# A first half's choice made earlier, a mixture's front reordered, and row loads six pairs ahead

## The reference, cut to what matters

```
x = layernorm(x + recurrent(x))            # a scan over time, sigmoid gate, projection
x = layernorm(x + cross_attention(x, ctx))
scores  = sigmoid(x @ w_gate.T)            # 16 experts in 4 groups
allowed = the 2 groups whose best two scores sum highest
idx     = top 4 experts among the allowed  # the choice
w       = scores[idx] / sum(scores[idx])
routed  = sum_k w_k * (silu(x @ w1[idx_k].T) * (x @ w3[idx_k].T)) @ w2[idx_k].T
shared  = (silu(x @ w1_s.T) * (x @ w3_s.T)) @ w2_s.T      # every token
out     = layernorm(x + routed + shared)
```

## Time and profile before

| what | value |
|---|---|
| timed runs | 1370.61, 1376.79, 1378.01 us (median 1376.79) |
| the profiled execution's own time | 1360.66 us |
| its span, first to last instruction | 1358.9 us |
| TensorE, mean granted clock over the span | 0.922 |
| busy: PE, DVE, ACT, POOL | 86%, 53%, 43%, 37% |

### The profile page before, as it was taken

One profiled execution on the slowest core, in us unless ns is written; L12 is line 12 of the kernel. 1 busy time (PEld: TensorE's weight loads), 2 busy tenths in 40 slices (PEclk: granted clock), 3 DMA queues, 4 the chain that ended last, 5 costly groups with the idle time before them and its releaser, 6 DMA issues. The chain is left out here.

```text
span 1358.9 us, 23999 instructions
## 1 busy us (share of the span) xinstructions
PE 1165.4 (86%) x7558; PEld 839.3 (62%) x7558; DVE 715.5 (53%) x1906; ACT 585.8 (43%) x1064; POOL 501.6 (37%) x924
## 2 busy tenths in 40 slices
PE   7589899899877967999999999995988676999970
PEld 3244344444344434889999999884555555998850
DVE  4767567676444644423223223285776636655564
ACT  1257677777765643223233233233333122556710
POOL 6333312331421331013333323112321278838856
PEclk9579999999998998999999999997999677999995
DMA  3980000000000007401111111032500024767633
GB/s 139 313 320 2 1 0 0 1 0 0 2 0 1 1 1 283 156 24 40 33 39 40 36 37 39 25 125 74 192 1 0 5 74 139 233 196 213 213 117 101
DMA packets 68127, 109.31 MB, mean 80 GB/s; under 512 B 7345, under 2 KB 54962, under 8 KB 65202
## 3 DMA queue, kind: packets, MB, share of 16 engines
q1 hardware_dynamic: 58130, 80.96, 17.4%
q0 software_dynamic: 9888, 27.01, 6.2%
HBM read 65.61 MB, written 42.34 MB: 79 GB/s over the span
## 5 line engine op out<-in xcount | busy, mean ns | idle before, releaser
L1391 ACT ACTIVATE f_work<-f_bank,f_ub 128x128 f32<-128x128 f32 x312 | 89.0, 368 | 204.3 <-PE f_bank L1713 204.3
L494 ACT ACTIVATE att_PT<-att_ST 128x1024 f32<-128x1024 f32 (+1 forms) x192 | 147.8, 809 | 66.3 <-PE att_ST L608 34.8
L527 DVE CUSTOM_DVE_ANT_0 att_junk<-att_RB,att_causal_q 128x128 f32<-128x128 f32 (+3 forms) x256 | 120.9, 487 | 60.7 <-PE att_RB L590 48.7
L1713 PEld LDWEIGHTS f_bank<-f_work,f_xTf 128*128 128x128 f32 x1248 | 145.4, 192 | 3.9 <-DVE f_work L1513 2.0
L1713 PE MATMUL f_bank<-f_work,f_xTf 128*128 128x128 f32 x1248 | 145.9, 276 | 1.5 <-DVE f_work L1513 1.5
L590 PE MATMUL att_RB<-att_kT,att_qT 96*128 96x512 bf16 (+3 forms) x384 | 122.0, 357 | 23.3 <-DVE att_mx L527 7.2
L1722 PE MATMUL f_bank<-wd_down,f_work 128*128 x624 | 141.2, 380 | 0.0
L1722 PEld LDWEIGHTS f_bank<-wd_down,f_work 128*128 128x128 f32 x624 | 115.8, 191 | 13.8
L1342 POOL DMA_INDIRECT Yd<-f_work,f_inv x39 | 38.5, 987 | 196.3 <-DVE f_work L1532 196.3
L1522 DVE COPY f_xTf<-wu_up 128x1024 f32 x78 | 54.1, 694 | 102.8 <-PE f_bank L1713 95.0
L590 PEld LDWEIGHTS att_RB<-att_kT,att_qT 96*128 96x128 bf16 x384 | 34.0, 99 | 115.9 <-issue 40.4
(11 more groups left out here) (456 smaller groups left out, 2230.9 us busy)
## 6 DMA issues: line engine op xcount, KB each, us to landing
Xd<-g_zero SPq DMA_DIRECT2D x1, 12032.0 KB, 38.4
f_xin<-Xd SPq DMA_DIRECT2D x47, 256.0 KB, 3.6
Yd<-f_yo SPq DMA_DIRECT2D x47, 256.0 KB, 2.2
wu_up<-up_w SPq DMA_DIRECT2D x9, 1024.0 KB, 14.4
wd_down<-down_w SPq DMA_DIRECT2D x9, 1024.0 KB, 18.4
w_all<-w SPq DMA_DIRECT2D x6, 768.0 KB, 10.8
wu_up<-Yd SPq DMA_DIRECT2D x16, 256.0 KB, 5.8
w_all<-w SPq DMA_DIRECT2D x1, 2304.0 KB, 17.3
```

The source lines that it names most:

```text
L494: act.activation(buf[:, :, 0:w], ST[:, 2 * (k % 2):2 * (k % 2) + 2, 0:w], ACT.Exp, scale=float(HD) ** -0.5).then_inc(exp_done, 1)
L527: dve.tensor_tensor_reduce(junk[:, k % RING, 0:w], RB[:, bank, 0:w], G.causal_q[:, 512 - w:512], 1.0, LOWEST, ALU.add, ALU.max, to).then_i ...
L1391: last = act.activation(hT[:, u % 2, m, :], bank[:, UB + m // 4, (m % 4) * P:(m % 4 + 1) * P], ACT.Gelu, bias=ub[:, ds(e, 1), m])
L1713: mm = pe.matmul(bank[:, UB + n, P * m:P * (m + 1)], staged_up[:, kk, at:at + P], xT[:, u % 2, kk, :], start=(kk == 0), stop=(kk == KD - 1))
```

## The change

The kernel computes the same. Work moves, and a few waits with it:

```diff
-    put(("r", 3, 1), ("tg", 0, 0), ("tg", 0, 1), ("tg", 1, 0), ("tg", 1, 1), ("lg", 0, 0))
-    put(("rs", 3, 1), ("c", 0, 0))
-    put(("y", 3, 1), ("c", 0, 1))
-    put(("tx", 3, 1), ("c", 0, 2))
-    put(("s", 3, 0), ("c", 0, 3), ("ct", 0, 0))
-    put(("dn", 3, 0), ("lc", 0, 0), ("sx", 0, 2))
+    put(("tx", 2, 1), ("tg", 0, 0), ("tg", 0, 1), ("tg", 1, 0), ("tg", 1, 1))
+    put(("v", 3, 1), ("lg", 0, 0), ("c", 0, 0), ("c", 0, 1), ("c", 0, 2), ("c", 0, 3))
+    put(("r", 3, 1), ("ct", 0, 0))
+    put(("rs", 3, 1), ("lc", 0, 0), ("sx", 0, 3))
+    put(("y", 3, 1), ("sx", 3, 13))
...
-    SCATTERS, SENT = TH * K, 2
+    SCATTERS, SENT = TH * K, 13
...
-            for q in range(N + NX):
+            LAG = 6
+            for q in range(N + LAG):
                 if q < N:
                     load(q)
-                if q >= NX:
-                    keep_result(q - NX)
+                if q >= LAG:
+                    keep_result(q - LAG)
...
+            for q in range(3):
+                stage(q)
             for m in range(2 * FIRST):
                 shared_silu(m)
-            for q in range(3):
-                stage(q)
...
-            dve.wait_ge(exp_done, 1)
-            for m in range(2 * FIRST):
-                shared_product(m)
-                route.choose(dve, ch, 1, m)
-            shared_sum(0)
-            dve.wait_ge(sums_ready, 1)
-            route.locate(dve, ch, 1, bank[:, SB_ + 1, 0:CE], bank[:, SB_ + 1, CE:2 * CE])
-            route.owners(dve, ch, 1)
-            shared_sum(1)
-            for n in range(HALVES):
-                route.weights_of(dve, ch, n)
...
             for q in range(3):
                 stage(q)
+            dve.wait_ge(exp_done, 1)
+            route.choose(dve, ch, 1, 0)
+            route.choose(dve, ch, 1, 1)
+            shared_product(0)
+            route.choose(dve, ch, 1, 2)
+            shared_product(1)
+            route.choose(dve, ch, 1, 3)
+            shared_product(2)
+            dve.wait_ge(sums_ready, 1)
+            route.locate(dve, ch, 1, bank[:, SB_ + 1, 0:CE], bank[:, SB_ + 1, CE:2 * CE])
+            shared_sum(0)
+            shared_product(3)
             take_x(0)
             take_x(1)
+            shared_sum(1)
+            route.owners(dve, ch, 1)
...
+                if q in (4, 6):
+                    route.weights_of(dve, ch, (q - 4) // 2)
...
                 if q >= 2:
                     pe.wait_ge(y_done, q - 1)
+                else:
+                    pe.wait_ge(sh_added, 2 * (FIRST - 1) + q + 1)
...
             shared_up(2)
+            count()
             shared_down(0)
             shared_up(3)
-            count()
-            shared_down(1)
             pe.wait_ge(sh_prod, 2 * FIRST)
-            pe.wait_ge(sh_added, 2 * FIRST)
-            pe.wait_ge(pos_ready, 2)
-
             turn_x(0)
             turn_x(1)
+            shared_down(1)
             up(0)
```

## The result

| | before | after |
|---|---|---|
| timed runs, median | 1374.31 us (4 runs, 1370.61 to 1378.01) | 1341.80 us (4 runs, 1341.20 to 1342.71) |
| the profiled execution's own time | 1360.66 us | 1341.20 us |
| its span, mean granted clock | 1358.9 us, 0.922 | 1339.4 us, 0.923 |

The ratio of the timed runs is 0.9763, with an interval of 0.9736 to 0.979: faster by 2.4%. The two ways of counting disagree: 32.5 us by the timed medians, 19.5 us by the profiled executions, for which the working had said 20.6.

The account below looks back on a forecast made before the run. Mixture 2's pair loop was taken to wait for POOL's scatter queue, then late loads. Terms -10.8 (including +1.7), -1.6 and -8.2 sum to -20.6 us: 1340.1 profiled, 1356 from the timed 1376.79; range 1345 to 1368.

Parts of the forecast that it names:

- Theory L: Experiments' theory: late loads cost the kernel before more in most executions than in the profiled one; the change removes that.
- Rival F: Experiments' rival to Theory L: the timed runs' excess over the profiled execution has nothing to do with the loads.
- 1, boundary later: Recurrent program: choosing ahead delays y(3), most is given back in the last quarter, and the end comes 1.7 us later.
- 3, up(0): Mixture 2's front: 11 fewer scatters after the boundary and TensorE ready in time bring up(0) 10.8 us sooner.
- 4, up(0) to third up: Start of the pair loop: TensorE stays warm, saving 1.6 us, or 0 if cold again.
- 5, loop: Pair loop: loads six pairs ahead in SP's program remove all eight stalls, saving 8.2 us.
- down(1) at the full clock: Front, now on the path: 3.6 us instead of 5.23; with turns also slow, up(0) gains only 8.6 us.
- Three staging copies beside the scatters: VectorE copies during first-half scatters: taken at nothing; by the skill's rule 1.7 us in all, 1358 us.
- A: Front gives little: part 1's 6.6 us not given back, lower clock stays; 1363 us, chance 0.13.
- B: Pair loop: contention with gathers keeps loads late, so 8.2 us stay; 1364 us, chance 0.10.
- D: Recurrent program: y(3) so late that it ends over 8 us later; some 1371 us, chance 0.04.
- C: POOL becomes the bound: 2.2 us slack remains, stretched first-half gathers eat the gain; 1384 us, chance 0.03.

Follow-up runs that it names:

- e7_lag3: The changed kernel with loads three pairs ahead of the stores instead of six: 1465.9 us, ratio 1.0767.
- c0_before: The kernel before, unedited, profiled again on another chip: 1361.8 us (one run).
- c3_before: The kernel before, unedited, timed against itself and profiled on a further chip: 1361.9 us against 1362.4.
- e1_lag_only: The kernel before with only the loads moved, six pairs ahead of the stores instead of four: 1358.4 us, ratio 0.9968.
- e4_after_no_drain: The changed kernel without POOL's drain between the two halves' gathers: 1345.1 us, ratio 0.9862 to the kernel before.
- e3_plan_only: The kernel before with the new places and 13 scatters in the recurrent program, mixture 2's front and loads as before: 1360.1 us, ratio 0.9991.
- e5_front_lag: The changed kernel's new front and loads six ahead, with the old places and 2 early scatters: 1361.1 us, ratio 0.9998 to the kernel before.
- e9_tail_drain: The changed kernel with an early drain before the first gather, spread(1) four gathers later, and a third drain behind the last gather: 1337.3 us.

## Why the prediction was wrong in its number and right in most of its steps

**The step that failed is the last one**: "I carry the difference over: 1376.79 - 20.6 = 1356". It took the 16 us between the kernel before's timed runs and its profiled execution for something that every kernel would have. The gap was 16.1 us in the one kernel (13.7 with the fourth run) and 0.6 in the other: the changed kernel's four timed runs lie 0 to 1.5 us above its profiled execution, and on the later chips the kernel before itself read 1360.0 to 1362.4, at most 1.7 us above the 1360.66 of that execution. Counted from the profiled execution, as the sum itself was, the forecast was 1340.1, and the measurement 1341.2 (profiled) and 1341.8 (timed). The range was hung on the same 1356 and ended at 1345. What made the first runs of the kernel before so long stays open. Theory L is at most half borne out: late loads vary by 6 us between executions and r(3) by 3, but they account for a level of 1374 in no run here. Rival F, a cause elsewhere, isn't shown either, since no later run had the excess; a ring like that of e7_lag3 might make such a level, but none was seen in the kernel before.

The steps of the sum, in the profiled execution:

| step | forecast | measured |
|---|---|---|
| 1, boundary later | +1.7 | +0.5 (1093.76 to 1094.30), +0.2 counted from k(2) |
| 1, places ready; x4(3) ends | 1061.8; 1074.3 | 1061.0 (first scatter 1061.84); 1073.4 |
| 3, up(0) | -10.8 | -12.2 (1142.63 to 1130.47) |
| 4, up(0) to third up | -1.6 | -1.5 (6.88 to 5.38) |
| 5, loop | -8.2 | -8.3 (143.64 to 135.37) |
| last up | -20.6 | -21.9 (1293.15 to 1271.22) |
| second half's first gather | the same | -16.4 (1300.27 to 1283.91) |
| last gather | the same | -19.5 (1348.60 to 1329.08) |

Step 1 was 1.2 us too dear in this pair of executions; against those with a slow r(3) the change gains about 3 us there. ACT's last steps of the changed kernel:

```profile
1090.18 1.09 ACT L2019 ACTIVATE g_x<-rx_xr,rx_shift,rx_rstd 128x256 f32<-128x256 f32 x2 [5.93 <-POOL rx_shift L1933]
1091.87 1.09 ACT L2019 ACTIVATE g_x<-rx_xr,rx_shift,rx_rstd 128x256 f32<-128x256 f32 x2 [0.59 <-POOL rx_shift L1933]
```

They end at 1092.96, forecast 1093.8. The ten scatters between the spreads cost nothing, as said. In step 3 the scores took 6.98 us instead of 4.19, at the lower clock (granted 0.50 instead of 0.88). That is no effect of the change: c0_before, c3_before and e1_lag_only have 6.98 too, six other executions 4.0 to 4.2. Nor did it cost anything. With quick scores the front is done before its rows, TensorE idles 3.72 us and goes on at a granted clock of 0.58, as its timeline in e4_after_no_drain shows:

```profile
1099.21 4.03 PE L2754 MATMUL f_bank<-w_gate,r_xTf 128*128 128x16 f32 x32 [0.87 <-DVE r_xTf L2630]
...
1126.11 1.73 PE L2793 MATMUL f_bank<-g_ident_f,f_xin 128*128 128x128 f32 x8 [3.72 <-DMA f_xin<-Xd]
1127.63 4.68 PE L2783 MATMUL f_bank<-w_all,f_hs 128*128 128x256 f32 x16
```

Turns and down(1) take 1.7 us more than in the changed kernel, and up(0) comes at 37.5 us instead of 36.2. down(1) at the full clock was a choice of the forecast (3.6 us against 5.23): the changed kernel has 3.62.

**Three staging copies beside the scatters** were taken at nothing. POOL's timeline where they run (VectorE at 1101.77, 1102.54 and 1103.32, 0.56 us each):

```profile
1100.76 0.97 POOL L2335 DMA_INDIRECT Xd<-g_x,r_pos  x1 [0.28 <-issue]
1102.14 1.09 POOL L2335 DMA_INDIRECT Xd<-g_x,r_pos  x1 [0.28 <-issue]
1103.63 1.09 POOL L2335 DMA_INDIRECT Xd<-g_x,r_pos  x1 [0.28 <-issue]
```

Two scatters are 0.12 us longer, 0.24 in all; e3_plan_only, which sends the same scatters and has no copies there, shows 0.97 and 0.96 in their place. By the rule of the Trainium skill (SBUF — State Buffer, "Who interferes with whom") up to three whole copies, 1.7 us, could have been lost; the trace shows 0.24.

**Rivals.** A and B did not happen: up(0) came at full speed and the loads are never late. The forecast named a wait of up(0) for VectorE's products as a sign of being wrong; the turns did wait 0.88 us for one, which its own sum had in it (product at 1126.2, turns at 1126.9). D neither. C, the other side, had the place right and the price wrong. I read the 9.75 us of idle POOL as slack and reckoned that 2.2 us of it would remain. It held a drain, which the row doesn't show because the stores came last: with the loads alone changed (e1_lag_only) the same place shows 8.56 us of which no other engine is the cause. The true slack was 1.2 us in that execution, and it varies with the late loads: c0_before has 8.56 us there and so none, c3_before 14.23 and so 5.7. POOL's gathers of the first half began 14.4 us sooner (1224.99 to 1210.61), the last up came 21.9 us sooner. Of the 7.5 us between the two, the slack took 1.2 and the cheaper drain 0.9 (7.66 for 8.56); the rest, 5.5, was lost at the second half's first gather; 3.1 came back, since POOL's 2.2 us wait for statistics behind the fourth gather had gone and the gathers ran slightly quicker. That the end came within 1.1 us of the sum is thus in part luck: 1.3 us more than forecast were won by the last up, and 2.4 us lost behind it. It was luck too that the sum started from a quick execution of the kernel before, such as the changed kernel's all are up to the boundary.

## What to carry to other kernels

Make the forecast from one and the same execution, and don't add a gap between timed runs and profile to another kernel: the gap may be the old kernel's own, or that day's. And profile the old kernel more than once: one execution doesn't tell which stretches vary. Before idle time is counted as slack, look up what instructions stand in it (drains and waits are no busy time); a wait is put down to the last one to end, and the second last may be just behind. Two edits that are worth nothing alone can be worth 12 us together, where one makes data early and the other makes its reader ready: price them as one.

## What the runs showed of the hardware

- A drain on GpSimd costs by what it has issued: 3.50 us with 32 indirect transfers since the drain before, 7.66 with 83 since the boundary between the programs, 8.56 with 94 (e1_lag_only, e5_front_lag). That is 0.082 us each plus 0.9, by both steps; the third drain of e9_tail_drain, with 32 again, took 3.1. It's an inference that the boundary starts the count. At the program's end the line is too high (5.5 us with 64, where it gives 6.1; 8.2 with 115, where it gives 10.3).
- A prefetch that is one pair too short is not one pair slower: six ahead 135.4 us of loop, four ahead 142 to 148, three ahead 265.
- A distance at the edge shows as scatter too: the loop took 142.3 to 148.2 us in six executions with four pairs ahead, and 135.37 or 135.38 in all ten with six.
- The same work at the same place can get either clock from one execution to the next: r(3) of the kernels with the old places took 3.70 us at a granted clock of 1.00, 5.40 at 0.67, or 6.5 to 6.63 at 0.54 to 0.55.
- A VectorE copy of 128x768 f32 (0.56 us) beside a scatter made it 1.09 us long instead of 0.97.
